# A graph kernel's gathers: a ring of 128 tiles in place of 64, and a wait four gathers back

## What is computed

```python
h = X * rsqrt(deg_out)                      # convolution
agg = segment_sum(h[src], dst) * rsqrt(deg_in)
out = batchnorm(relu(agg @ W) + relu(X @ Wres))
...
h = x @ W_enc.T + b_enc                     # message network
for l in range(2):
    m = relu(concat(h[row], h[col]) @ W1[l].T + b1[l]) @ W2[l].T + b2[l]
    agg = segment_sum(m, col)
    h = layer_norm(h + concat(h, agg) @ upd_W[l].T + upd_b[l])
return h @ W_out.T + b_out
```

## Time and profile before

| | us |
|---|---|
| three runs | 4050.43, 4048.61, 4035.29 |
| median | 4048.61 |
| the profiled execution, its span | 4035.4 |
| PE / DVE / ACT / Pool busy | 3232.4 / 2736.0 / 2365.9 / 1721.0 |
| gathers of the degrees stage (L900, 344) | 329.0 busy |
| gathers of both edge stages (L900, 784) | 762.8 busy |

### The profile page before, as it was taken

One profiled execution on the slowest core, in us unless ns is written; L12 is line 12 of the kernel. 1 busy time (PEld: TensorE's weight loads), 2 busy tenths in 40 slices (PEclk: granted clock), 3 DMA queues, 4 the chain that ended last, 5 costly groups with the idle time before them and its releaser, 6 DMA issues. The chain is left out here.

```text
span 4035.4 us, 93659 instructions
## 1 busy us (share of the span) xinstructions
PE 3232.4 (80%) x25704; PEld 2882.7 (71%) x25704; DVE 2736.0 (68%) x8732; ACT 2365.9 (59%) x5642; POOL 1721.0 (43%) x1684
## 2 busy tenths in 40 slices
PE   5989945655447789956999878999749998789998
PEld 3744424555443389956998878999749988779998
DVE  9988855655448988844766546666426665458888
ACT  3779933655442278843665544666426665447888
POOL 0000044666640033345455563555454555636553
PEclk9999977876669999977999988999869999889999
DMA  0047732443219999964665433999736654328887
GB/s 18 2 163 255 254 123 64 118 103 89 77 49 372 395 330 386 386 237 131 194 189 175 146 105 106 325 325 330 268 102 191 191 175 150 115 73 258 262 261 220
DMA packets 461027, 778.11 MB, mean 193 GB/s; under 512 B 113722, under 2 KB 115898, under 8 KB 460726
## 3 DMA queue, kind: packets, MB, share of 16 engines
q1 hardware_dynamic: 379958, 594.21, 43.8%
q0 software_dynamic: 37632, 77.15, 7.5%
q10 hardware_dynamic: 43136, 102.98, 7.3%
HBM read 439.00 MB, written 334.88 MB: 192 GB/s over the span
## 5 line engine op out<-in xcount | busy, mean ns | idle before, releaser
L932 DVE SCALAR_TENSOR_TENSOR edges_acc<-edges_acc,keep,edges_ps_a 128x128 f32 (+1 forms) x2352 | 819.6, 348 | 389.5 <-issue 129.1
L900 POOL DMA_INDIRECT ring<-table_p,esrc x784 | 762.8, 973 | 626.6 <-PE edges_ps_m L1023 334.1
L1022 PE MATMUL edges_ps_m<-ring,ident 128*128 x3136 | 645.5, 287 | 143.3 <-issue 118.1
L1023 PE MATMUL edges_ps_m<-edges_q_ring,edges_turned 128*128 x3136 | 633.4, 283 | 51.3 <-issue 51.0
L917 DVE TENSOR_TENSOR edges_onehot<-iota,drel 128x512 f32<-128x512 f16 x441 | 303.2, 688 | 499.9 <-DMA table_p<-nodes_p_out 320.2
L990 ACT ACTIVATE edges_msg<-edges_ps_m 128x512 f32<-128x512 f32 x392 | 231.7, 591 | 662.8 <-DMA nodes_in_z<-table_z 226.6
L1022 PEld LDWEIGHTS edges_ps_m<-ring,ident 128*128 128x128 f32 x3136 | 497.9, 199 | 165.4 <-issue 140.0
L1023 PEld LDWEIGHTS edges_ps_m<-edges_q_ring,edges_turned 128*128 128x128 f32 x3136 | 499.2, 199 | 62.5 <-issue 61.9
L1047 PE MATMUL edges_ps_a<-ring,edges_onehot 128*128 x1568 | 307.4, 370 | 263.7 <-ACT edges_onehot L958 88.7
L1032 PE MATMUL edges_ps_a<-edges_onehot,edges_msg 128*128 128x128 f32 x3136 | 436.6, 284 | 79.3 <-issue 77.8
L1047 PEld LDWEIGHTS edges_ps_a<-ring,edges_onehot 128*128 128x128 f32 x1568 | 279.4, 272 | 291.6 <-ACT edges_onehot L958 113.5
(11 more groups left out here) (310 smaller groups left out, 7022.7 us busy)
## 6 DMA issues: line engine op xcount, KB each, us to landing
table_z<-nodes_z_t SPq DMA_DIRECT2D x196, 256.0 KB, 5.4
table_p<-nodes_p_out SPq DMA_DIRECT2D x196, 256.0 KB, 4.3
table_q<-nodes_q_out ACTq DMA_DIRECT2D x196, 256.0 KB
edges_q_ring<-table_q SPq DMA_DIRECT2D x196, 256.0 KB
edges_d_ring<-table_d ACTq DMA_DIRECT2D x98, 512.0 KB
table_t<-edges_acc SPq DMA_DIRECT2D x196, 256.0 KB
nodes_in_a<-table_t SPq DMA_DIRECT2D x196, 256.0 KB
nodes_in_z<-table_z SPq DMA_DIRECT2D x196, 256.0 KB, 4.3
```

The source lines that it names most:

```text
L900: nc.gpsimd.indirect_dma_start(out=ring[:, e % RE * W:e % RE * W + P], out_offset=None, in_=table[:, :], in_offset=bass.IndirectOffsetOnAx ...
L932: nc.vector.scalar_tensor_tensor(out=to, in0=to, scalar=m.keep[:, s:s + 1], in1=ps_a[:, i % AR, where(j):where(j) + F], op0=ALU.mult, op1= ...
L1022: nc.tensor.matmul(to, m.ident[:], rows[j], start=True, stop=False)
L1023: last = nc.tensor.matmul(to, turned[:, i % QR, j * P:(j + 1) * P], slots[j], start=False, stop=True)
```

## The change

The ring gets 128 places, and a tile lies in place (e + 4) % 128. The row word's low 9 bits now hold e + 4 of the batch's last step. From them PE takes both the number of groups that must have landed, (e + 4) // 4, and the last step's place; the other three steps have fields of 7 bits above. Pool's wait for PE (L897) is for group g - 32 and so begins at group 32. Every gather from the fifth of a stage on waits for `s_issued`, which each gather raises by one when Pool itself has ended it (not when its data has landed): at most four gathers are handed over and not ended. The 48 gathers in the plan stage carry the same wait. To make room, seven arrays of the rank and place stages become parts of one (`m.spare`), in which the plan stage also puts its weights and two rows, and the plan's DVE chain writes over arrays that it has read.

```diff
-RE = 64
+RE = 128
+SHIFT = 4
+QUEUED = 4
@@ plan_stage
-        row_n = sb("row_n", [P, 1 + TP])
-        sen_row = sb("sen_row", [P, 1 + TP])
+        row_n = m.spare[:, 14 * P:14 * P + 1 + TP]
+        sen_row = m.spare[:, 18 * P:18 * P + 1 + TP]
-        wt, spread = sb("wt", [P, 9, P]), sb("spread", [P, 5, P])
+        wt = m.spare[:, 0:9 * P].rearrange("p (k d) -> p k d", k=9)
+        spread = m.spare[:, 9 * P:14 * P].rearrange("p (k d) -> p k d", k=5)
...
                 for e in range(PRE):
+                    if e >= QUEUED:
+                        pool.wait_ge(s_issued, e - QUEUED + 1)
                     nc.gpsimd.indirect_dma_start(
-                        out=m.ring[:, e * W:e * W + P], ...).then_inc(s_row, 16)
+                        out=m.ring[:, (e + SHIFT) * W:(e + SHIFT) * W + P], ..., engine_sem=s_issued).then_inc(s_row, 16)
...
-                nc.vector.tensor_scalar(ik(2), ik(0), RE - 1, None, ALU.bitwise_and)
                 nc.vector.tensor_scalar(ik(3), ik(1), 4 * RC - 1, None, ALU.bitwise_and)
-                nc.vector.tensor_scalar(ik(4), ik(0), 2, None, ALU.arith_shift_right)
+                nc.vector.tensor_scalar(ik(4), ik(0), SHIFT, None, ALU.add)
                 link(nc.vector.tensor_scalar(ik(5), ik(1), 2, None, ALU.arith_shift_right))
-                nc.vector.tensor_scalar(ik(7), ik(4), 1, None, ALU.add)
-                link(nc.vector.tensor_scalar(ik(8), ik(5), 1, None, ALU.add))
+                nc.vector.tensor_scalar(ik(2), ik(4), RE - 1, None, ALU.bitwise_and)
+                link(nc.vector.tensor_scalar(ik(6), ik(5), 1, None, ALU.add))
...
-                pack(table[:, :, 0], 6, [of(7, 3)] + [of(2, j) for j in range(4)], 7)
-                pack(table[:, :, 1], 5, [of(8, 3)] + [of(3, j) for j in range(4)], 7)
+                pack(table[:, :, 0], 7, [of(4, 3)] + [of(2, j) for j in range(3)], 9)
+                pack(table[:, :, 1], 5, [of(6, 3)] + [of(3, j) for j in range(4)], 7)
@@ edge_stage, Pool
                     for j in range(4):
                         e = 4 * g + j
+                        if e - 4 * first >= QUEUED:
+                            pool.wait_ge(s_issued, e - 4 * first - QUEUED + 1)
                         nc.gpsimd.indirect_dma_start(
-                            out=ring[:, e % RE * W:e % RE * W + P], ...).then_inc(s_row[g % RG], 16)
+                            out=ring[:, (e + SHIFT) % RE * W:(e + SHIFT) % RE * W + P], ..., engine_sem=s_issued).then_inc(s_row[g % RG], 16)
@@ edge_stage, PE
                 def due(i):
-                    return [nc.tensor.compute_val(word[0][i % 2 * 2 + k] & 127) for k in range(2)]
+                    rows, slots = word[0][i % 2 * 2:i % 2 * 2 + 2]
+                    return [nc.tensor.compute_val((rows & 511) // 4), nc.tensor.compute_val(slots & 127)]
 
                 def row(i, j):
-                    return ring[:, bass.ds(word[0][i % 2 * 2] // (1 << (7 + 6 * j)) % 64 * W, F)]
+                    return ring[:, bass.ds(word[0][i % 2 * 2] // (1 << (9 + 7 * j if j < 3 else 0)) % RE * W, F)]
@@ build
-        m.v1, m.v2, m.src_low, m.src_high, m.pos, m.pos_low, m.pos_high = (
-            sb(n, [P, TP]) for n in ("v1", "v2", "src_low", "src_high", "pos", "pos_low", "pos_high"))
+        m.spare = sb("spare", [P, 7 * TP])
+        m.v1, m.v2, m.src_low, m.src_high, m.pos, m.pos_low, m.pos_high = (m.spare[:, k * TP:(k + 1) * TP] for k in range(7))
```

## The result

The changed kernel is slower: 4196.4 us (median of 4 runs, 4189.5 to 4212.2) against 4044.4 beside it (4 runs, 4035.3 to 4050.4), ratio 1.038; what stands in brackets behind a ratio, here [1.036, 1.040], is its 95% interval. The profiled execution took 4189.5 us with a span of 4187.7, 152 longer than the 4035.4 of before.

What follows compares the result with a forecast made beforehand. The edge stages were taken as bound by freezes from unbroken gathers, not by lacking rows. Terms -94 (edge stages), 0 (degrees), -10 (plan), -1 (step words) sum to -105: 3930 profiled, 3943 us as median; range 3840 to 4190.

Steps and rivals of the forecast that it cites:

- What bounds the kernel: Edge stages: while gathers run unbroken, engines' end-of-work signals arrive many us late (a freeze), losing 142 us a stage.
- The ring alone is a loss: Edge-stage opening: 128 places add 80 us of freeze, in which PE does 2 or 3 batches, against 20 gained.
- The wait: Gathers: at most four stand, so a freeze stops its own cause if Pool's own signal is late in it.
- I take late: Pool's end-of-gather signal in a freeze: assumed late as PE's and DVE's are, 5.9 to 20 us; called the weak step.
- the -94 us of the edge stages: Both edge stages together: each falls from 716 to 669 us, -47 apiece.
- the rival: Whole kernel: Pool's signal is prompt, the wait never holds, openings freeze longer; +119 us, 4168 us, chance 0.37.
- Degrees: Degrees stage: 0 change taken, between +34 at 1.63 us a gather and -97 at 1.25.
- Plan and step words: Plan stage: -10 us from shorter DVE stalls under the wait; step words: -1 us from less packing and indexing.
- The rule of four gathers in 6.5 us: Edge stages: the fastest pace that leaves PE whole, 1.63 us a gather.
- The stage of 649 us: Edge stage bound by Pool: 392 gathers at 1.63 us make 639, plus about 10 for the last tiles.
- 1, the depth of the queue: Pool's queue: its depth causes the freeze, four standing gathers freeze nobody; -397 us, 3652 us, chance 0.10.
- 2, the freezes spread over the stage: Edge stages: opening freezes spread at the dense pace, so no change; 4040 us, chance 0.11.

Runs made afterwards that it cites:

- e5: The kernel before with a Pool memset of 128x256 behind every gather of the three gathering stages, pace 1.445 us; ratio 0.994.
- e6: The kernel before with a Pool fill of 128x512 behind every gather of the three gathering stages, pace 1.66 us; ratio 0.989.
- e13: The kernel before with a Pool fill of 128x352 behind every gather of the three gathering stages; 3879.8 us against 4083.0, ratio 0.951.
- e18: The kernel before (ring of 64) with a Pool fill of 128x416 behind every gather of the gathering stages; ratio 0.965.
- e9: The kernel before with a ring of 32 tiles and 32 gathers issued ahead in the plan in place of 48; ratio 0.995.
- e3: The kernel before with each gather, in the plan too, waiting for Pool's end of the one right before it; ratio 1.000.
- e8: The kernel before with gathers of the three gathering stages fetching 64 of a row's 128 values, half the bytes; ratio 1.001.
- e16: The kernel before with each gather of the three gathering stages fetching 64 rows in place of 128; ratio 1.007.
- e7: The kernel before with a Pool fill of 128x1024 after every fourth gather of the gathering stages; ratio 0.956.
- e14: The kernel before with a 128x1024 fill after every fourth gather in only the first 16 groups of each gathering stage; ratio 0.995.
- e12: The changed kernel (ring of 128) without its wait, with a 128x1024 fill after every fourth gather; ratio 1.018.
- e17: The changed kernel (ring of 128) without its wait, with a 128x416 fill after each gather; ratio 0.965.

## Why the prediction was wrong

The forecast was 3943 us, faster; it was slower and 6 us above the range's upper end. Point by point:
- *What bounds the kernel* was read right: the freeze in the openings, tied to how Pool issues gathers and not to rows that lack. e5, e6, e13 and e18 show it by spacing them, e9 by the length of the run. "Unbroken" was not quite the word: with a fill behind each gather Pool is as busy as ever, and what counts is the distance between gathers.
- *The ring alone is a loss*: right in sign. The opening grew by 89 and 86 us for the 72 said (80 less 3 batches); the tail gave back some 35 for the 20 said. Net +56 and +50 for +52.
- *The wait. The step that failed: "I take late".* From PE's and DVE's late signals I took Pool's own to be late as well. In the changed kernel 110 gathers that each wait for such a signal, of four gathers back, start 0.3 us behind the end of the one before, and in e3_queue1 even the signal of the gather right before is back in 0.3 us. So the wait never held, and the -94 us of the edge stages became +106. The trace of before had a contrary sign: Pool's landing counts kept coming in the freeze. I had put it down for the rival and let two other engines outweigh it. The rival had it right in every place but one.
- *Degrees* was that one: 0 in the forecast, +15 in the rival, +50 measured. The opening (80 gathers before the ring is full, for 16) cost 88 us, by which DVE's accumulations are behind those of before from the 60th on, near the 80 said; the 64 gathers fewer gave back only 38 of the 98 I had credited: the stage issued as many gathers as before, in 523 us for 527, since the rest went at the pace of the one-hots, which the freeze had put behind. That is the term that I had mis-sized for the rival. Of the 147 one-hots that I put beside the gathers, 138 were beside them and 9 behind the earlier trace rows; nothing hung on it.
- *Plan and step words*: -5 for -10 and -1. DVE's two stalls stayed: 14.1 us before L698, where the kernel before has 15.5.
- *The rule of four gathers in 6.5 us*, at which PE is whole, was on the safe side: at 1.575 us it is whole too. The stage of 649 us worked out from that rule is what e18 gives (649 and 650), but with a pace that fills force and not the wait, and with a second half in which PE waits for rows; that the numbers agree is in part luck.
- *Rivals*: 1, the depth of the queue, is refuted by e3. 2, the freezes spread over the stage, did not occur: the first 180 us of each stage held it in one piece.

## What to carry to other kernels

A deeper buffer in front of an engine lets its feeder run ahead for longer. Ask first what that run does to the others, and whether the consumer lacks data at all. When a trace shows signals that come late, don't carry the lateness over from one engine to another: find a row in which the engine that is to wait gets its own signal in the same stretch. Where issuing disturbs the others, a little more time between issues (here 0.3 us) can be worth more than depth (none of the rings of 32, 64 and 128 places came near it), and it has to be measured step by step: 1.445 us gave 0.994, 1.525 gave 0.951, 1.575 gave 0.965, 1.66 gave 0.989.

## What the runs showed of the hardware

- While Pool issues indirect gathers every 1.25 us, the end of a batch's last matmul on PE reaches ACT up to 20.7 us late (19.9 us in the kernel before, 20.6 in the changed one, 20.7 in e3), and PE's own matmuls start 1.7 us and more apart. Pool's own signal is back in 0.3 us (e3). Neither half the bytes (e8) nor half the rows (e16) changes it; at 1.445 us it is partly gone, at 1.575 and 1.66 us the openings are free (29 messages in 92 us). What in the chip does it, no run here tells.
- It is not fixed by Pool's instructions alone: the same ones gave 22 batches in 92 us in e7's opening and 13 in e14's, on two occasions. Fully frozen openings ended only once the ring was full, at 32, 64 and 128 places; in e12 a freeze once ended with places free.
- A gather costs Pool nearly the same for 64 rows as for 128 (0.90 and 0.95 us).
- The granted clock in the frozen openings is 0.50 to 0.54 of full speed, so mostly at the lower level of 1.2 GHz, with PE 11 to 22% busy; in the free openings of e6, e17 and e18 it is 0.91. The matmuls of a frozen opening stand 1.7 us and more apart, at 0.37 us each, so it is not the clock that holds them.
